# Attention scores by fp32 row tiles against bfloat16 splits through DRAM, in a kernel of two attentions and two MLPs

## The chip, the cores and the metric

The kernel runs on one core of a Trainium2 chip. Its engines run in parallel and meet by semaphores: TensorE (PE in the profile) multiplies into PSUM, which has 8 banks of 128 partitions x 512 fp32 numbers; VectorE (DVE), ScalarE (ACT) and GpSimd (POOL) work on tiles of 128 partitions; the DMA engines move data, and here nearly all DMAs are issued by SyncE (SP, its queue SPq). The metric is the device time of one execution in microseconds; lower is better. It was measured three times: 398.62 us (median), 397.15 us and 402.47 us.

## The reference

There are 16 batches of 128 rows x 256 numbers. Each goes through two rounds of attention and feed-forward, with a layer norm ahead of each part:

```python
x = x + _L0_xattn_ref(_layernorm(x), ctx, ctx)      # 16 heads of 16 numbers, causal, 128 queries x 128 keys
x = x + _L0_ffn_ref(_layernorm(x), ...)             # 256x256 layer plus the 2 best of 8 experts of rank 16
x = x + _L1_xattn_ref(_layernorm(x), ctx, ctx, g)   # 8 heads over the 128 rows as features, 256 queries x 256 keys
x = x + _L1_ffn_ref(_layernorm(x), w1, w2, gamma)   # 256 -> 1024, gelu, -> 256, activations rounded to 8 bits
```

Both attentions are softmax(q k / 4) v in fp32. Their scores need more precision than one bfloat16 product gives.

## The kernel before

Every batch b passes the same stages: attention 0, expert layer ("moe"), attention 1, MLP. The program is a pipeline over iterations t. The table of constants at the top (S0, S1T, EXP1 and so on) says how many iterations after its first one a batch reaches a stage, so that in iteration t each engine works on some ten batches at different stages. In every iteration an engine walks its own hand-written list (`fill` for t below 8, `body` to 15, `drain` after), and within that order only semaphores hold it back. One wait that isn't met holds all that stands behind it on the same engine.

**Scores.** Each fp32 operand is split into three bfloat16 parts. For k, POOL does four operations per batch (`k_high`, `k_rest_`, `k_mid`, `k_low`); for q, ACT makes a rounded and a full copy of the normalised rows and POOL takes the rests. The parts go out to DRAM (`k_parts`, `q0_parts`, `q1_parts`) and come back stacked, six parts of a head's 16 rows on 96 partitions (`load_stack`), so that one bfloat16 matmul over 96 rows gives the score of one head to nearly fp32 precision. `scores0` and `scores1` (L1166, L1197) compute scores with queries on the partitions, of which DVE takes row maxima (`maxima0`, `maxima1`, L1851). The negated maxima are split in two parts, turned by PE, copied by ACT and written by two DMAs (`rows0`, `rows1`, L755 and L764) as rows 96 and 97 of the stacked q, against two rows of ones in the stacked k. `scores0_t` and `scores1_t` (L1182, L1213) then compute the scores again with keys on the partitions and the maxima already subtracted, ACT takes the exponential into p (L1555, L1565), POOL sets the part above the diagonal to 0 in attention 0 (L920), and PE multiplies by v with an added column of ones (`pv0`, `pv1`, L1227, L1244). The causal mask is added to `scores0` by one bfloat16 matmul of 512 columns (L1162).

**PSUM.** A unit of scores is one bank, 512 columns wide; per batch there are 4 units in attention 0 and 8 in attention 1, in each of the two directions. `ps_s` has two banks and `ps_st` has two, used in turn, so PE can fill one while DVE or ACT reads the other.

**Tiles of TensorE.** The products by v have 32 output columns (L1227, L1244 say 128*32: rows*columns of the array), four such matmuls writing to four groups of 32 partitions. All other matmuls use the whole array.

**MLP.** Its stages have offsets of 16 to 31 iterations: layer-norm statistics and quantisation of the input (`stats3_` to `copy_in`), `up` (L1465), gelu (L1786), its maximum (L2274), rounding (`round_hid` L1796, `quant_hid` L2302), `turn_hid`, `copy_hid`, `down` (L1492), scaling and adding. The first gelu comes after the last exponential; ACT then loads its other function table once.

**Loads.** SP starts with x and kv of the first two batches, then the constants; the MLP weights are loaded by ACT's queue in iterations 4 and 6, the rest of x by ACT in iterations 0 to 5.

## Time and profile before

The profiled execution has a span of 399.2 us from its first to its last instruction, against the median of 398.62 us over the runs.

| | PE | DVE | ACT | POOL |
|---|---|---|---|---|
| busy, us | 306.1 | 315.5 | 262.4 | 271.7 |
| share of the span | 77% | 79% | 66% | 68% |

The DMA engines moved 56.21 MB at a mean of 141 GB/s. A busy engine is not an engine at its peak: a matmul's record lasts until its results are in PSUM, and the next one streams in behind it. "Idle before" is an engine's idle time just ahead of a group, with what released it. PEld is the loading of weights into the array, which runs beside matmuls.

### The profile page before, as it was taken

How to read it: one execution, taken by the hardware profiler on the slowest of the kernel's cores; microseconds unless marked ns; L12 is line 12 of the kernel's file. 1: busy time of each engine (PE TensorE's matmuls, PEld its weight loads, DVE VectorE, ACT ScalarE, POOL GpSimd, SP SyncE). 2: the span in 40 equal slices, each digit the busy share in tenths (PEclk: the TensorE clock that was granted, in tenths of full speed). 3: DMA queues.
4: the chain of work that ended last, by engine and by line, in shares of the span. 5: the costliest groups of instructions: out<-in, count | busy, mean ns of one | idle time of the engine just before them, and what ended most of it. 6: DMA issues, size and time to landing. Idle time of an engine off the chain costs nothing.

```text
span 399.2 us, 9590 instructions
## 1 busy us (share of the span) xinstructions
PE 306.1 (77%) x2926; PEld 192.0 (48%) x2946; DVE 315.5 (79%) x841; ACT 262.4 (66%) x501; POOL 271.7 (68%) x508
## 2 busy tenths in 40 slices
PE   0355665867989999898898899998777866767884
PEld 0233543654655656556555465555344432444553
DVE  6543579589898889899895889987797657999993
ACT  2422434636766887869576786596457548997993
POOL 5763988988988898699996795654542133756555
PEclk9999589869899999999998999999898889698998
DMA  5777768875866569567775667523444000000112
GB/s 185 188 222 225 185 168 253 240 177 159 187 183 201 153 180 251 152 196 175 203 218 129 187 160 203 132 64 84 96 108 118 14 16 1 0 16 29 40 54 79
DMA packets 73138, 56.21 MB, mean 141 GB/s; under 512 B 5376, under 2 KB 62592, under 8 KB 73088
## 3 DMA queue, kind: packets, MB, share of 16 engines
q1 hardware_dynamic: 69888, 51.67, 48.4%
q10 hardware_dynamic: 3200, 3.93, 3.3%
q8 instruction: 24, 0.39, 0.4%
q14 instruction: 26, 0.21, 0.2%
HBM read 36.45 MB, written 18.87 MB: 139 GB/s over the span
## 4 chain that ended last, share of the span: by engine, by line
PE 28%; POOL 19%; DVE 15%; issue 14%; DMA 12%; SPq 6%; ACT 4%; POOLq 1%; ACTq 0%; DVEq 0%
PE ps_u L1244 6%; DMA q<-max_t 5%; DVE max L1851 5%; PE ps_st L1213 4%; DMA kv_in<-in_kv 3%; PE ps_s L1197 3%; PE ps_ff L1314 3%; SPq L628 2%; POOL p L920 2%; POOL xs L1116 2%; PE ps_st L1182 2%; DMA k_parts<-k_split 2%; POOL rstd L970 2%; DVE hq L2302 1%; POOL k_split L853 1%
## 5 line engine op out<-in xcount | busy, mean ns | idle before, releaser
L1851 DVE TENSOR_REDUCE max<-ps_s 128x2 f32<-128x512 f32 (+1 forms) x192 | 127.0, 682 | 33.6 <-PE ps_s L1166 17.0
L1565 ACT ACTIVATE p<-ps_st 128x512 f32<-128x512 f32 x128 | 71.7, 599 | 18.7 <-PE ps_st L1213 16.9
L1213 PE MATMUL ps_st<-q,k 98*128 98x256 bf16 x256 | 47.9, 284 | 9.4 <-DMA q<-max_t 4.7
L1197 PE MATMUL ps_s<-k,q 96*128 96x256 bf16 x256 | 50.2, 283 | 5.4 <-DVE max L1851 2.5
L920 POOL TENSOR_SCALAR_AFFINE_SELECT p<-p 128x512 f32<-128x512 f32 x64 | 39.7, 636 | 8.1 <-ACT p L1555 8.0
L1555 ACT ACTIVATE p<-ps_st 128x512 f32<-128x512 f32 x64 | 35.6, 601 | 13.1 <-PE ps_st L1182 12.3
L1244 PE MATMUL ps_u<-p,v 128*32 128x256 f32 x512 | 38.0, 419 | 5.7 <-POOL v L910 5.7
L1213 PEld LDWEIGHTS ps_st<-q,k 98*128 98x128 bf16 x256 | 20.1, 100 | 31.5 <-DMA q<-max_t 9.2
L1166 PE MATMUL ps_s<-k,q 96*128 96x128 bf16 x256 | 27.2, 232 | 7.2 <-POOL p L920 6.4
L1569 ACT ACTIVATE q_split<-xs,shift,rstd 128x256 bf16<-128x256 f32 (+1 forms) x32 | 22.7, 711 | 12.4 <-POOL shift L972 8.1
L1081 POOL TENSOR_SCALAR amax_c<-amax,rms 128x1 f32<-128x1 f32 x16 | 4.9, 305 | 37.4 <-DVE amax L2256 37.3
L1182 PE MATMUL ps_st<-q,k 98*128 98x128 bf16 x256 | 27.2, 249 | 4.0 <-DMA q<-max_t 3.6
L1197 PEld LDWEIGHTS ps_s<-k,q 96*128 96x128 bf16 x256 | 20.8, 101 | 18.2 <-DVE max L1851 8.2
L1314 PE MATMUL ps_ff<-wff_sb,xh_t 128*128 128x392 f32 x64 | 26.5, 539 | 1.3 <-DVE w_mean L2098 0.8
L1166 PEld LDWEIGHTS ps_s<-k,q 96*128 96x128 bf16 x256 | 21.7, 105 | 9.9 <-issue 3.3
L1227 PE MATMUL ps_u<-p,v 128*32 128x128 f32 x512 | 25.2, 286 | 1.5 <-POOL p L920 1.3
L1182 PEld LDWEIGHTS ps_st<-q,k 98*128 98x128 bf16 x256 | 21.2, 113 | 9.4 <-DVE k L2154 3.0
L853 POOL TENSOR_SCALAR k_split<-kv_in 128x1024 bf16<-128x1024 f32 x14 | 14.6, 1045 | 16.2 <-DMA kv_in<-in_kv 9.1
L1342 PE MATMUL ps_t<-ident_bf,q_split 128*128 128x128 bf16 x128 | 13.3, 265 | 15.5 <-POOL q_split L943 15.5
L1244 PEld LDWEIGHTS ps_u<-p,v 128*32 128x32 f32 x512 | 14.4, 117 | 21.4 <-issue 10.3
L1796 ACT ACTIVATE hr<-hid,round_all,qscale 128x1024 f32<-128x1024 f32 x16 | 20.5, 1284 | 2.7 <-DVE qscale L2293 2.7
L1786 ACT ACTIVATE hid<-ps_s,dequant 128x512 f32<-128x512 f32 x32 | 20.8, 720 | 1.9 <-PE ps_s L1465 1.6
(144 smaller groups left out, 800.3 us busy)
## 6 DMA issues: line engine op xcount, KB each, us to landing
k_parts<-k_split SPq DMA_DIRECT2D x16, 512.0 KB, 4.8
k<-k_parts SPq DMA_DIRECT2D x32, 256.0 KB, 3.6
q<-q_parts SPq DMA_DIRECT2D x32, 256.0 KB, 4.0
kv_in<-in_kv SPq DMA_DIRECT2D x16, 256.0 KB, 3.9
q_parts<-q_t SPq DMA_DIRECT2D x16, 256.0 KB, 3.5
k<-k_parts SPq DMA_DIRECT2D x32, 128.0 KB, 3.6
q<-q_parts SPq DMA_DIRECT2D x32, 128.0 KB, 4.0
q_parts<-q_split SPq DMA_DIRECT2D x16, 256.0 KB, 3.1
```

Source lines behind the costliest of these rows:

```text
L920: pool.affine_select(out=kept, in_=kept, compare_op=ALU.is_ge, fill=0.0, base=0, pattern=[[0, G], [1, P]], channel_multiplier=-1).then_inc ...
L1166: last = pe.matmul(out_[:, j * P:(j + 1) * P], q0[0:STK, odd, c:c + P], k0[0:STK, odd, c:c + P], start=False, stop=(j == G - 1), skip_grou ...
L1182: last = pe.matmul(out_[:, j * P:(j + 1) * P], k0[0:STM, odd, c:c + P], q0[0:STM, odd, c:c + P], start=(j == 0), stop=True, skip_group_che ...
L1197: last = pe.matmul(out_[:, f * D:(f + 1) * D], q[0:STK, odd, h * D + f * P:h * D + (f + 1) * P], k[0:STK, odd, h * D:(h + 1) * D], start=( ...
L1213: last = pe.matmul(out_[:, f * D:(f + 1) * D], k[0:STM, odd, h * D + f * P:h * D + (f + 1) * P], q[0:STM, odd, h * D:(h + 1) * D], start=( ...
L1227: last = pe.matmul(ps_u[32 * j:32 * j + 32, g * P:(g + 1) * P], v0[:, odd, h, :], p0[:, g, j * P:(j + 1) * P], start=True, stop=True, skip ...
L1244: last = pe.matmul(ps_u[32 * j:32 * j + 32, g * D:(g + 1) * D], v1[:, f * H1 + h, :], p1[:, h, f * D:(f + 1) * D], start=(f == first), sto ...
L1314: last = pe.matmul(ps_ff[:, 0:NFF], xh1_t[:, f, :], wff_sb[:, f, :], start=(f == 0), stop=(f == FT - 1), skip_group_check=True)
L1555: act.activation(p0[:, g, :], ps_st[bank_of(ST_BANKS, f"s0t{g}")][:, :], ACT.Exp, scale=SCALE).then_inc(exp0_done[g], 1)
L1565: act.activation(p1[:, h, :], ps_st[bank_of(ST_BANKS, f"s1t{h}")][:, :], ACT.Exp, scale=SCALE).then_inc(exp1_done[h], 1)
L1569: return act.activation(out_, in_, ACT.Identity, scale=scale, bias=shift)
L1851: dve.tensor_reduce(out_, src, AX.X, ALU.max, negate=True).then_inc(done, 1)
```

## The change

The kernel is rewritten around one idea, and its parts are:

- **No splits.** q and k stay fp32. The array is used as four tiles of 32 rows x 128 columns. A row group of 32 partitions holds two heads; k has zeros where the other head's rows would be, so that one matmul over 32 rows with 256 columns gives the scores of two heads. The zeros are set once per buffer by DVE (`zero_k0`, `zero_k1`). `k_parts`, `q0_parts`, `q1_parts`, their stores and loads, and all of POOL's, ACT's and DVE's split operations on q and k are gone.
- **Loads of k.** `load_k0` and `load_k1` copy k from the input by 8 DMAs per batch each, of 16 partitions, on SP's queue.
- **Maxima.** They are still split in two (now by POOL), turned and copied, but are added from `max0_t` and `max1_t` by a bfloat16 matmul of 2 rows x 512 columns per bank; no DMA carries them.
- **Units of two banks.** `ps_s` and `ps_st` are each one buffer of two banks, 1024 columns. Per batch and direction there are 2 units in attention 0 and 4 in attention 1; maxima, exponentials and masks are 1024 wide. `claim` makes PE wait until the reader of the last unit is done with both banks.
- **Pairs.** `together` interleaves a transposed unit on two of the row groups with a plain unit of another batch on the other two.
- **Moved work.** x1, the index conversion and pick2 go from DVE to POOL. The MLP input stages of batches 0 to 12 are done between attentions.
- **MLPs in three groups.** Batches 0 to 5 after the scores of batch 13, 6 to 11 after the last exponential, and then 12 to 15, with hidden and input tiles in 7 buffers each.
- **Order and loads.** All iterations are written out. All loads are on SP: kv of three batches, x of the first, the constants, both MLP weights, the rest of x, and then k.

```diff
-        ps_s = [bank(f"ps_s{i}", [P, G * P]) for i in range(2)]
-        ps_st = [bank(f"ps_st{i}", [P, G * P]) for i in range(2)]
+        ps_s = bank("ps_s", [P, HALF, BANK])
+        ps_st = bank("ps_st", [P, HALF, BANK])
...
-            sp.dma_start(view[0:RUN], first_rows(parts)).then_inc(landed, 16)
-            sp.dma_start(view[RUN:STK], second_rows(parts, slot)).then_inc(landed, 16)
...
+                for i in range(I):
+                    for e in range(E):
+                        rows = slice(i * R + e * DH, i * R + (e + 1) * DH)
+                        sp.dma_start(k0[rows, n, :, e, :],
+                                     kv[b, rows, 0, :].rearrange("p (f l) -> p f l", f=FT)).then_inc(k0_landed[n], 16)
...
+            def together(*streams):
+
+                moved = {s: 0 for s in streams}
+                while moved:
+                    least = min(moved, key=moved.get)
+                    columns = next(least, None)
+                    if columns is None:
+                        del moved[least]
+                    else:
+                        moved[least] += columns
...
+            def scores0(b, h):
+                n = b % K0_BUFS
+                claim("s")
+                for m in range(HALF):
+                    pe.matmul(ps_s[:, m, :], ident_bf[:, :], mask_q[:, :, :].rearrange("p g k -> p (g k)"), start=True,
+                              stop=False, skip_group_check=True)
+                pe.wait_ge(k0_landed[n], (b // K0_BUFS + 1) * I * E * 16)
+                pe.wait_ge(q0_copied, b + 1)
                 for f in range(FT):
...
+                    for m in range(HALF):
+                        i = h * HALF + m
+                        rows = slice(i * R, (i + 1) * R)
+                        last = pe.matmul(ps_s[:, m, f * D:(f + 1) * D], q0[rows, b % Q_BUFS, f, :],
+                                         k0[rows, n, f, :, :].rearrange("p e l -> p (e l)"), start=False, stop=True,
+                                         skip_group_check=True)
...
+            def scores1_t(b, k, h):
+                n = b % K1_BUFS
+                claim("st")
+                pe.wait_ge(max1_copied, b + 1)
+                for e in range(E):
+                    for m in range(HALF):
+                        i = h * HALF + m
+                        rows = slice(i * R, (i + 1) * R)
+                        pe.matmul(ps_st[:, m, e * D:(e + 1) * D], k1[rows, n, e, k * P:(k + 1) * P], q1[rows, b % Q_BUFS, :],
+                                  start=(e == 0), stop=True, skip_group_check=True)
+                    yield D
+                for m in range(HALF):
+                    i = h * HALF + m
+                    pe.matmul(ps_st[:, m, :], ones_bf[i * R:i * R + 2, :],
+                              max1_t[i * R:i * R + 2, :, :, :].rearrange("p e f q -> p (e f q)"), start=False, stop=True,
+                              skip_group_check=True).then_inc(st1_ready[k][h], 1)
+                hold("st", (exp1_done[k][h], b + 1))
+                yield P
```

PE's order in the middle of the program before, at the start of an iteration of `body` (p and v are the probabilities and values, ps_u their product, ps_ut the turned product, ps_t the bank of small transposes):

```order
L1197 MATMUL ps_s0<-k1,q1 128x256 x2
L1244 MATMUL ps_u<-p1,v1 32x256 x8
L1213 MATMUL ps_st0<-q1,k1 128x256 x2
L1256 MATMUL ps_ut<-ident,u0 128x128 x4
L1213 MATMUL ps_st1<-q1,k1 128x256 x2
L1353 MATMUL ps_t<-ident,a1 128x128 x2
L1197 MATMUL ps_s1<-k1,q1 128x256 x2
L1213 MATMUL ps_st0<-q1,k1 128x256 x2
```

The same engine in the middle of the changed program, from the start of one batch's product by v (L1038 is `scores1`, L1019 and L1024 `scores0_t`, L1064 `scores1_t`, L984 and L992 `scores0`, L1101 `pv1`, L1164 the expert layer):

```order
L1164 MATMUL ps_ff<-wff_sb,xh1_t 128x392 x2
L1101 MATMUL ps_u<-p1,v1 32x256 x8
L1019 MATMUL ps_st<-q0,k0 128x128 x2
L1038 MATMUL ps_s<-k1,q1 128x512 x2
L1019 MATMUL ps_st<-q0,k0 128x128 x6
L1024 MATMUL ps_st<-max0_t,ones_bf 128x512 x2
L1051 MATMUL ps_t<-ident_bf,max1_split 128x128 x4
L1101 MATMUL ps_u<-p1,v1 32x256 x8
L1019 MATMUL ps_st<-q0,k0 128x128 x2
L1038 MATMUL ps_s<-k1,q1 128x512 x2
```

Units of one bank in alternating buffers became units of both banks in one buffer, and between two units stand matmuls on other tile shapes.

SP's queue at the start of the program before, up to the second batch's q:

```order
L652 DMA base_b_all<-in_base_b 128x256
L652 DMA wff_sb<-in_w_ff 128x2x392
L652 DMA router_b_all<-in_router_b 128x8
L676 DMA k_parts<-k_split 128x2x1024
L652 DMA lora_b_sb<-in_lora_b 128x256
L652 DMA attn_gamma_all<-in_attn_gamma 128x1
L652 DMA mlp_gamma_all<-in_mlp_gamma 128x256
L685 DMA q0_parts<-q0_t 128x1024
L627 DMA k0<-k_parts 64x8x256
```

The same queue in the changed program, from the weights on:

```order
L370 DMA w1_sb<-in_w1 128x1024 x2
L370 DMA w2_sb<-in_w2 128x4x256 x2
L320 DMA xs<-in_x 128x256
L320 DMA xs<-in_x 128x2x256 x2
L320 DMA xs<-in_x 128x4x256
L320 DMA xs<-in_x 128x6x256
L343 DMA k0<-in_kv 16x2x128 x24
L329 DMA kv_in<-in_kv 128x512 x3
L359 DMA k1<-in_kv 16x256 x40
L343 DMA k0<-in_kv 16x2x128 x16
```

The k of the first batch, which followed kv and some of the constants, now stands behind all weights and all of x, and the k of batch 3 (the first 8 of the last row) behind 24 + 3 + 40 other DMAs that follow x.

## Rows read from the trace of the kernel before

**Rows 1.** The page: busy time, share of the span and instructions of each engine:

```profile
PE 306.1 (77%) x2926; PEld 192.0 (48%) x2946; DVE 315.5 (79%) x841; ACT 262.4 (66%) x501; POOL 271.7 (68%) x508
```

**Rows 2.** Busy time (instructions) by stretch of the span, clock, DMA share, GB/s:

```profile
core 0: us, PE busy (x) PEld busy (x) DVE busy (x) ACT busy (x) POOL busy (x), PEclk, DMA share, GB/s
0.00:20.00 20.00, 3.29 (x23) 2.27 (x24) 12.45 (x28) 6.59 (x10) 13.13 (x36) 1.00 0.68 186
20.00:80.00 60.00, 38.56 (x361) 26.70 (x364) 35.15 (x86) 25.37 (x51) 45.21 (x75) 0.86 0.76 215
116.00:250.00 134.00, 122.93 (x1328) 78.14 (x1329) 116.04 (x326) 104.14 (x208) 109.17 (x183) 0.99 0.70 187
331.00:399.00 68.00, 46.54 (x364) 29.85 (x358) 57.59 (x134) 55.58 (x93) 39.52 (x86) 0.91 0.09 32
```

**Rows 3.** Single lines: count, shortest/median/longest ns, first and last start:

```profile
L1166 PE MATMUL ps_s<-k,q x256: 217/218/314, 19.1 to 256.3; 96*128 96x128 bf16 x128
...
L1197 PE MATMUL ps_s<-k,q x256: 269/273/421, 79.5 to 318.7; 96*128 96x256 bf16 x128
...
L1658 ACT COPY u<-ps_u x16: 577/587/588, 116.3 to 331.5; 128x512 f32<-128x512 f32 x16
...
L1658 ACT COPY u<-ps_u x6: 577/587/588, 147.9 to 231.5; 128x512 f32<-128x512 f32 x6
...
L1786 ACT ACTIVATE hid<-ps_s,dequant x32: 677/690/830, 335.1 to 387.1; 128x512 f32<-128x512 f32 x32
```

**Rows 4.** The page: the chain that ended last, share of the span by engine:

```profile
PE 28%; POOL 19%; DVE 15%; issue 14%; DMA 12%; SPq 6%; ACT 4%; POOLq 1%; ACTq 0%; DVEq 0%
```

**Rows 5.** Groups by form: count | busy us, mean ns | idle before, releasers:

```profile
L1851 DVE TENSOR_REDUCE max<-ps_s 128x2 f32<-128x512 f32 x128 | 84.9, 683 | 16.5 <-PE ps_s L1197 16.2
L1565 ACT ACTIVATE p<-ps_st 128x512 f32<-128x512 f32 x128 | 71.7, 599 | 18.7 <-PE ps_st L1213 16.9 <-issue 0.2
...
L1796 ACT ACTIVATE hr<-hid,round_all,qscale 128x1024 f32<-128x1024 f32 x16 | 20.5, 1284 | 2.7 <-DVE qscale L2293 2.7
L2274 DVE TENSOR_REDUCE amax<-hid 128x1 f32<-128x1024 f32 x16 | 19.2, 1202 | 0.6 <-ACT hid L1786 0.4
```

**Rows 6.** PE in time: start, us, line, array rows*columns, shapes, count:

```profile
206.04 0.38 PE L1162 MATMUL ps_s<-mask_q,ident_bf 128*128 128x512 bf16 x1
206.25 0.39 PE L1166 MATMUL ps_s<-k,q 96*128 96x128 bf16 x4
206.57 0.67 PE L1227 MATMUL ps_u<-p,v 128*32 128x128 f32 x16
207.17 0.60 PE L1314 MATMUL ps_ff<-wff_sb,xh_t 128*128 128x392 f32 x1
...
217.42 0.60 PE L1268 MATMUL ps_ut<-ident,u 128*128 128x128 f32 x4
```

**Rows 7.** PE in time: sixteen records of the second product by v:

```profile
129.08 1.07 PE L1244 MATMUL ps_u<-p,v 128*32 128x256 f32 x16
```

**Rows 8.** SP queue in time: start, us that the issue took, transfer:

```profile
8.91 1.10 SPq L652 DMA_DIRECT2D mlp_gamma_all<-in_mlp_gamma  x1
...
12.57 0.69 SPq L627 DMA_DIRECT2D k<-k_parts  x1
13.32 0.61 SPq L628 DMA_DIRECT2D k<-k_parts  x1
...
205.46 0.35 SPq L649 DMA_DIRECT2D kv_in<-in_kv  x1
```

**Rows 9.** The DMAs of the maxima rows: shortest/median/longest ns of an issue:

```profile
L755 SPq DMA_DIRECT2D q<-max_t x32: 548/580/689, 24.2 to 259.9; - x32
```

**Rows 10.** The page: GB/s of the DMA engines in 40 slices:

```profile
GB/s 185 188 222 225 185 168 253 240 177 159 187 183 201 153 180 251 152 196 175 203 218 129 187 160 203 132 64 84 96 108 118 14 16 1 0 16 29 40 54 79
```

**Rows 11.** ACT in time, late in the MLPs:

```profile
378.05 1.34 ACT L1786 ACTIVATE hid<-ps_s,dequant 128x512 f32<-128x512 f32 x2
...
380.95 1.37 ACT L1786 ACTIVATE hid<-ps_s,dequant 128x512 f32<-128x512 f32 x2
```

More of the change, by code:

```diff
@@ L33 @@
 FT = D // P
+R = 32
+I = P // R
+HALF = I // 2
+E = R // DH
+BANK = 512
 NE = 8
@@ L256, in kind @@
-def kind(t):
-    return 1 if not isinstance(t, int) or FILL <= t < NB else 0 if t < FILL else 2
-def in_turn(units, b, back=0):
-    stages, orders = units
-    which = [kind(b - back + stage) if isinstance(b, int) else 1 for stage in stages]
-    return sorted(range(len(stages)), key=lambda n: (stages[n], orders[which[n]].index(n)))
+X_GROUPS = ((0, 1), (1, 2), (2, 4), (4, 6), (6, 10), (10, NB))
+KV_BUFS = 3
+K0_BUFS = 3
+K1_BUFS = 5
+V0_BUFS = 3
+V1_BUFS = 5
+Q_BUFS = 2
+XN_BUFS = 4
+XR_BUFS = 3
@@ L536, in program @@
         xq_copied = sem("xq_copied")
-        hid_ready = sem("hid_ready")
+        hid_ready = [sem(f"hid_ready{n}") for n in range(2)]
         gelu_done = [sem(f"gelu_done{n}") for n in range(2)]
@@ L590, in claim @@
-        def claim(engine, bank):
-            for sem_, value in held.get(bank, ()):
-                engine.wait_ge(sem_, value)
-        def take(engine, order, banks, user, t):
-            bank_ = order[0][0], [name for name, _ in order].index(user) % banks
-            if isinstance(t, int):
-                claim(engine, bank_)
-            else:
-                name, last = before(order, banks, user, t)
-                engine.wait_ge(freed[name], last + 1)
-            if isinstance(t, int):
-                held[bank_] = ((freed[user], t - dict(order)[user] + 1),)
@@ new lines, in _ @@
+            turn_gated(3)
+            pv0(5, 0)
+            pv0(5, 1)
+            together(scores1_t(1, 0, 0), scores1(2, 1, 1))
+            turn_u0(5)
+            turn_q0(7)
+            together(scores1_t(1, 1, 0), scores0(6, 1))
+            lora(3)
+            turn_back(0)
+            together(scores1_t(1, 1, 1), scores1(2, 1, 0))
+            turn_max0(6)
+            ff(4)
+            pv1(1, 0)
+            together(scores0_t(6, 1), scores1(3, 0, 0))
+            turn_max1(2)
+            pv1(1, 1)
@@ new lines, in _ @@
+            turn_gated(6)
+            pv0(8, 0)
+            pv0(8, 1)
+            together(scores1_t(4, 0, 0), scores1(5, 1, 1))
+            turn_u0(8)
+            turn_q0(10)
+            together(scores1_t(4, 1, 0), scores0(9, 1))
+            lora(6)
+            turn_back(3)
+            together(scores1_t(4, 1, 1), scores1(5, 1, 0))
+            turn_max0(9)
+            ff(7)
+            pv1(4, 0)
+            together(scores0_t(9, 1), scores1(6, 0, 0))
+            turn_max1(5)
+            pv1(4, 1)
```

3823 lines of the change are left out of this document (2267 added, 1556 removed).

## The prediction

> **What bounds the kernel now.** First the page's busy shares: PE 77%, DVE 79%, POOL 68%, ACT 66% of 399.2 us [rows 1]. No engine is full, and the chain that ended last is shared out, PE 28%, POOL 19%, DVE 15%, DMA 12%, waits for issues 14% [rows 4]. So nothing bounds it alone; look by stretch [rows 2]. Until 80 us PE is busy for 42 of 80 us while the DMA engines move 186 to 215 GB/s, and no slice of the page has more than 253 [rows 11]: a fill held by transfers and POOL. From 116 to 250 us PE is busy 92% and DVE 87%. From 331 us there are only MLPs, 68 us.
>
> Three markers divide the time [rows 3]: `scores0` first runs at 19.1, `scores1` at 79.5, and ACT copies the second product by v (u, once per batch) at 116.3 for the first batch and 331.5 for the last. Six starts of it between 147.9 and 231.5 are five periods: 16.7 us per batch in the full pipeline. The first gelu is at 335.1.
>
> How long PE streams is read from spacing, not from mean ns. Four bfloat16 matmuls of 128 columns occupy 206.25 to 206.64 with their tail of .17, so .055 each, one column per cycle at 2.4 GHz [rows 6]. Sixteen records of 256 columns in fp32 take 1.07 us [rows 7]. They are 8 matmuls of two records each, on four column tiles. Four records per tile in (1.07 - .17) / 4 = .22 us each is two cycles per column, and the four tiles run side by side. So an fp32 matmul of N columns costs 4N cycles, .43 us for 256, .86 for 512.
>
> **The change, part by part.**
>
> Scores on PE. Before, a batch has 12 units in each of two directions, 512 bfloat16 columns each, .21: 24 x .21 = 5.1 us. After, it has 6 units of two banks per direction. In a pair each of the four row groups streams 512 fp32 columns, .86, and one bfloat16 matmul of 512 for the maxima, .21: 1.07 if the four run side by side, as the column tiles do. Six pairs are 6.4 us. The masks are .86 (two units x 2 x .21). So PE's scores cost 1.5 to 2 us more per batch, for half as many instructions. No row shows row tiles; the bounds are below.
>
> A rule speaks against the 1.07: the Trainium skill, "TensorE: Matmul & The Clock Gate", Part 3, reports 3.07 times, not 4, for four row tiles with K = 32 and 512 columns. By it the .86 would be an estimated 4 x .86 / 3.07 = 1.12, and 81 pairs would add 21 us. No run here shows it yet, and the sum does not use it.
>
> Switches of tile shape. Between the last 128-row matmul and the first column tile PE pauses about .10 (206.47 to 206.57), and back again .17 (207.00 to 207.17) [rows 6]. Before there are about 5 per batch. In the new order one steady iteration passes between row tiles, column tiles and the whole array 18 times. At .16 that is 2.9 us.
>
> The rest of PE's iteration: `pv1` 1.7 and `pv0` .9, the expert layer 1.3 (2 x .327 x 2 for 392 columns), turning u .9, lora .4, turns of xh, a and q .65, gated .1, maxima .4: 6.4 us. Sum: 6.4 + .9 + 6.4 + 2.9 = 16.6 us of PE per batch.
>
> One buffer instead of two. PE may start a unit only when its reader has finished both banks. DVE's maximum over 1024 columns takes 1.20 (the row of that size), against 2 x .68; ACT's exponential of 1024 between 2 x .60 and, by the form of that width, 1.28 [rows 5]. From a pair's last column to the next pair's first: .17 tail + 1.20 + .1 = 1.45 us. Pair plus hand-over is 2.5 us, so PE cannot take fewer than 6 x 2.5 = 15.1 per batch. PE's other work, (16.6 - 6.4) / 6 = 1.7 per pair, would cover 1.45 if spread evenly; it is not: `pv1`, the expert layer and the turns stand in three of six gaps. I charge half a microsecond in each of the other three: 1.5. A steady iteration is 16.6 + 1.5 = 18.1 us, against 16.7. Bounds: 15.6 (hand-over alone, with half a microsecond of slack) and 20.
>
> What is taken from others. DVE goes from 12 maxima at .68 to 6 at 1.20 and gives x1 and index work to POOL; POOL gives up the splits; ACT the copies. DMA traffic falls from 56 MB to some 15 (an estimate: inputs, kv of each batch twice, output). I cost all this at nothing in the middle, because PE's own iteration is longer than theirs, and it gives nothing either. Without that cover DVE's 7 us of maxima plus the rest still stay under 14.
>
> SP's queue in the fill. The first k0 stands behind kv, the constants, both weights and x, 5.6 MB. At the best rate seen, 253 GB/s, that is 22 us, plus issue of 8 DMAs and 2 us of flight: first scores at 26 (19.1 before). Then SP issues 24 + 3 + 40 + 8 DMAs before the k of batch 3 is complete. Issues over 128 partitions take .35 [rows 8]; those of other shapes .61 and .69 (same rows), of the 16-partition maxima .58 [rows 9]; behind a backlog 1.10. With 16 partitions the nearest is .58, plus .06 between: .64. 72 x .64 + 3 x .4 = 47 us after 19.5: k of batch 3 is there at 67. PE reaches it after 10 units that are not in pairs; each is 1.07 plus 1.45 of hand-over of which units in the other direction cover some, I take 2.2: at 26 + 22 = 48. So PE, whose list is in one order, stands for 19 us, and behind it everything.
>
> From 67 on: 7 units of 2.9 (18.1 / 6 is 3.0, the fill has fewer pairs): first `scores1` at 87 (before 79.5); 9 units to the first `pv1` at 113 (before about 115); 6 units, 17 us, to the second at 130; nine full iterations to `pv1` of batch 10: 9 x 18.1 = 163, at 293. Then 25 units, 13 of them pairs, of 2.7: 361.
>
> MLPs. The first group of six stands before that: 12 gelus that PE, ACT and DVE would otherwise do later, and two more changes of ACT's function table; the hand-over units run on, so I charge only part of it: 18 us. Last `pv1` at 379 (before 331.5). Behind it stand 10 MLPs, not 16. Late in the program a batch takes 2.9 us (378.05 to 380.95) [rows 10]: 10 x 2.9 = 29, plus 12 for the way of the last batch through all stages, 41 (before 68).
>
> Sum: 26 + 22 + 19 + 20 + 26 + 17 + 163 + 68 + 18 + 41 = **420 us**. The profile is of 399.2 against a median of 398.62, so nothing is to be corrected.
>
> **Rivals.**
>
> *Faster (about 375).* Hand-over alone sets the pace, 15.6 us, because PE's small work fits the gaps; switches cost .05. For it: PE only needs 13.7 without switches, and all other engines get lighter. Then 9 x 2.5 = 22 less, the late units 2.4 instead of 2.7, 8 less, and with cheap issues 17 less: 373. It decides on the faster side once an iteration is below 16.5 with a short stall. Chance .22.
>
> *Within 2% (391 to 407).* The small DMAs are issued in .39 like those of 128 partitions. Then k of batch 3 is there at 19.5 + 72 x .39 + 1 + 2, about 50, and the stall of 19 is 2: 403. Or the stall stands and an iteration is 16.8. Against it: every row of fewer than 128 partitions says .58 or more. Chance .18.
>
> *Row tiles less parallel (470 to 495).* If only two run at once, 81 pairs cost 1.07 more: 420 + 87, less what hand-overs hide, 495. If their weights are loaded one after another, a pair with 20 loads of .1 has 1 us exposed in half of the cases, 460. Against it: column tiles are fully parallel [rows 7]. Chance .12.
>
> *As forecast, 407 to 450:* .48.
>
> **How the numbers follow.** The forecast is 420, the likeliest case. The range leaves out part of the fast and most of the row-tile case: 383 to 462. 2% is about what a measurement of this kernel can tell from no change. Faster .22, same .18, slower .48 + .12 = .60.
>
> **What would show it.** SP's rows for k0 and k1: issue near .6 or near .4, and PE's idle time ahead of the `scores0` of batch 3. The period of the u copy in the middle: 18.1, and its parts: records of a pair (1.07 side by side), the gaps where the tile shape changes, and PE's idle time ahead of `ps_s` and `ps_st`, put down to DVE's maximum or ACT's exponential. First `scores0` at 26, `scores1` at 87, last u copy at 379. I am wrong if PE is seldom idle and the period is below 16.7, if the stall is short, or if the row groups' records follow one another.

## The result, and the profile after

The changed kernel takes 428.01 us (median of 5 runs, 423.12 to 429.85) against 401.35 us for the kernel before, measured beside it: a ratio of 1.068, with a 95% interval of 1.058 to 1.077. Medians here and below are of all executions, while ratios and their intervals leave out executions in the chip's slower state, more than 1.5% above the fastest of their kernel. The forecast was 420. The profiled execution is the shortest of the five (423.12 us) and has a span of 421.3 us; all stretches below are of it, and the forecast's sum compares with its 421.3.

From the page of the changed kernel: busy shares, the chain's shares, and the groups of the exponential and the maximum.

```profile
PE 347.9 (83%) x3634; PEld 205.3 (49%) x3634; DVE 284.5 (68%) x633; ACT 238.8 (57%) x375; POOL 188.2 (45%) x436
...
PE 63%; ACT 13%; issue 8%; SPq 6%; DVE 6%; POOL 2%; DMA 1%; ACTq 0%; POOLq 0%; DVEq 0%
...
L1744 ACT ACTIVATE p<-ps_st 128x1024 f32<-128x1024 f32 x64 | 65.5, 1024 | 78.0 <-PE ps_st L1069 78.0
L2210 DVE TENSOR_REDUCE max<-ps_s 128x4 f32<-128x1024 f32 x64 | 78.3, 1223 | 41.5 <-PE ps_s L1038 40.6
```

PE is now the busiest engine by far (83%, where [rows 1] had 77%) and 63% of the chain, against 28% in [rows 4]. DVE, ACT and POOL all have less work than before, and the kernel is slower all the same. The same views of single lines as in [rows 3] (count, shortest/median/longest ns, first and last start): `scores0`, `scores1`, the copy of the second product by v (u) over the whole run and within 140 to 240 us, and SP's loads of the first attention's k.

```profile
L992 PE MATMUL ps_s<-k,q x256: 374/374/792, 23.7 to 287.6; 32*128 32x256 f32 x128
...
L1038 PE MATMUL ps_s<-k,q x256: 587/662/1052, 79.6 to 356.6; 32*128 32x512 f32 x128
...
L1753 ACT COPY u<-ps_u x16: 576/603/604, 107.8 to 378.3; 128x512 f32<-128x512 f32 x16
...
L1753 ACT COPY u<-ps_u x6: 603/603/604, 144.6 to 239.3; 128x512 f32<-128x512 f32 x6
...
L343 SPq DMA_DIRECT2D k<-in_kv x128: 311/423/1999, 15.1 to 244.7; - x128
```

And the stretches, with the columns of [rows 2]:

```profile
0.00:24.00 24.00, 1.86 (x6) 0.92 (x8) 10.03 (x25) 3.06 (x5) 8.20 (x30) 1.00 0.74 250
24.00:60.00 36.00, 27.25 (x190) 15.94 (x188) 22.20 (x42) 12.57 (x16) 13.39 (x26) 1.00 0.18 51
...
291.00:374.00 83.00, 73.14 (x711) 43.22 (x709) 59.55 (x136) 59.21 (x92) 30.55 (x77) 0.98 0.04 11
```

The period of the u copy in the middle is (239.3 - 144.6) / 5 = 18.94 us, where [rows 3] give 16.7. By the same copy the two profiled executions compare as follows. The first copy comes 8.5 us earlier (107.8 against 116.3). The ten periods behind it take 185.5 us against 159.7, and the last five, among which the first group of MLPs now stands, 85.0 against 55.5. Behind the last copy (378.3 against 331.5) stand 43.0 us instead of 67.7. Together that is 22.1 us more.

| step | forecast | measured |
|---|---|---|
| first `scores0` | 26 | 23.7 |
| to that of batch 3 | 41 (22, and a stall of 19) | 36 |
| to the first `scores1` | 20 | 20 |
| to the first `pv1` | 26 | 23 |
| to the second | 17 | 19 |
| nine iterations | 163 | 169 |
| to the last `pv1` | 86 (68 + 18) | 83 |
| rest | 41 | 47 |
| sum | 420 | 421 |

The first seven rows go by PE's starts of the score units and of `pv1`. For its last `pv1` the prediction's 379 took over a marker of [rows 3] that is the start of the u copy (331.5 before); by that marker it was 378.3, with 43 us behind it, against 379 and 41.

One pair in the middle shows what an iteration is made of. The rows are of PE, DVE and ACT (weight loads left out); the pair runs from 207.33 to 208.61, where a full-array transpose starts.

```profile
207.33 0.48 PE L1064 MATMUL ps_st<-q,k 32*128 32x256 f32 x2
...
207.47 0.70 PE L1038 MATMUL ps_s<-k,q 32*128 32x512 f32 x2
...
208.01 0.59 PE L1038 MATMUL ps_s<-k,q 32*128 32x512 f32 x2
...
208.61 0.66 PE L1113 MATMUL ps_ut<-ident,u 128*128 128x128 f32 x4
208.74 1.23 DVE L2210 TENSOR_REDUCE max<-ps_s 128x4 f32<-128x1024 f32 x1 [1.32 <-PE ps_s L1038]
208.83 1.02 ACT L1744 ACTIVATE p<-ps_st 128x1024 f32<-128x1024 f32 x1 [0.81 <-PE ps_st L1069]
...
209.91 0.70 PE L1064 MATMUL ps_st<-q,k 32*128 32x256 f32 x4 [0.42 <-ACT p L1744]
210.54 0.61 PE L984 MATMUL ps_s<-mask_q,ident_bf 128*128 128x512 bf16 x2
...
212.14 0.70 PE L1181 MATMUL ps_ff<-lora_b_sb,gated_t 128*128 128x256 f32 x2
...
213.49 0.48 PE L1064 MATMUL ps_st<-q,k 32*128 32x256 f32 x2 [0.43 <-ACT p L1744]
...
222.69 0.70 PE L1064 MATMUL ps_st<-q,k 32*128 32x256 f32 x4 [0.40 <-ACT p L1680]
```

Two units on four row groups stand in 1.28 us, a gap of .10 at the change of tile shape included. DVE reads `ps_s` from 208.74 for 1.23 us, ACT reads `ps_st` from 208.83 for 1.02. PE has .9 us of other work, waits .42 for ACT, and starts the next transposed unit at 209.91. The mask matmul of the plain unit that is paired with it starts at 210.54. It does not wait for DVE, whose maximum ended at 209.97: it stands behind the transposed unit's first four records in PE's list. That pair, with its masks, takes 2.23 us (209.91 to 212.14). There are three waits per iteration, .40 to .43 each, and all three are for ACT's exponential.

### The profile page after: what moved, and what is told of

It is laid out like the page before. It is cut to its first block, busy times and chain, and to the rows that moved or that the text cites. A ratio compares the mean times of both kernels' runs of the same rounds, so it can differ in the third digit from the quotient of the medians.

```text
span 421.3 us, 10475 instructions
## 1 busy us (share of the span) xinstructions
PE 347.9 (83%) x3634; PEld 205.3 (49%) x3634; DVE 284.5 (68%) x633; ACT 238.8 (57%) x375; POOL 188.2 (45%) x436
## 4 chain that ended last, share of the span: by engine, by line
PE 63%; ACT 13%; issue 8%; SPq 6%; DVE 6%; POOL 2%; DMA 1%; ACTq 0%; POOLq 0%; DVEq 0%
PE ps_st L1064 11%; PE ps_u L1101 7%; PE ps_s L992 7%; ACT p L1744 6%; PE ps_st L1019 6%; PE ps_s L1038 6%; PE ps_ff L1164 5%; PE ps_s L984 4%; PE ps_u L1086 4%; ACT p L1680 3%; PE ps_st L1069 3%; SPq L343 3%; ACT hid L1788 2%; PE ps_u L1223 2%; SPq L320 1%
## 5 line engine op out<-in xcount | busy, mean ns | idle before, releaser
L1744 ACT ACTIVATE p<-ps_st 128x1024 f32<-128x1024 f32 x64 | 65.5, 1024 | 78.0 <-PE ps_st L1069 78.0
L2210 DVE TENSOR_REDUCE max<-ps_s 128x4 f32<-128x1024 f32 x64 | 78.3, 1223 | 41.5 <-PE ps_s L1038 40.6
L1064 PE MATMUL ps_st<-q,k 32*128 32x256 f32 x512 | 78.3, 411 | 16.7 <-ACT p L1744 11.9
L1038 PE MATMUL ps_s<-k,q 32*128 32x512 f32 x256 | 72.9, 644 | 1.8 <-DVE max L2210 1.8
L2201 DVE TENSOR_REDUCE max<-ps_s 128x8 f32<-128x1024 f32 x32 | 39.2, 1225 | 41.6 <-PE ps_s L992 41.6
L1064 PEld LDWEIGHTS ps_st<-q,k 32*128 32x128 f32 x512 | 42.4, 184 | 32.9 <-ACT p L1744 22.3
L992 PE MATMUL ps_s<-k,q 32*128 32x256 f32 x256 | 41.9, 450 | 12.7 <-DMA k<-in_kv 12.7
L1680 ACT ACTIVATE p<-ps_st 128x1024 f32<-128x1024 f32 x32 | 32.8, 1024 | 28.0 <-PE ps_st L1024 28.0
L508 POOL TENSOR_SCALAR_AFFINE_SELECT p<-p 128x1024 f32<-128x1024 f32 x32 | 35.2, 1101 | 16.6 <-ACT p L1680 16.6
L1019 PE MATMUL ps_st<-q,k 32*128 32x128 f32 x512 | 41.3, 303 | 1.4 <-ACT p L1680 1.2
L1019 PEld LDWEIGHTS ps_st<-q,k 32*128 32x128 f32 x512 | 34.5, 203 | 11.1 <-ACT p L1680 6.0
L992 PEld LDWEIGHTS ps_s<-k,q 32*128 32x128 f32 x256 | 24.8, 209 | 30.1 <-issue 15.2
L1101 PE MATMUL ps_u<-p,v 128*32 128x256 f32 x512 | 33.6, 384 | 0.0
L1164 PE MATMUL ps_ff<-wff_sb,xh_t 128*128 128x392 f32 x64 | 24.8, 510 | 0.0
L984 PE MATMUL ps_s<-mask_q,ident_bf 128*128 128x512 bf16 x64 | 22.0, 430 | 2.3 <-DVE max L2201 2.3
L1223 PE MATMUL ps_u<-w_q,hq_t 128*128 128x256 bf16 x128 | 16.7, 273 | 6.3 <-DVE hq_t L2436 4.8
L1038 PEld LDWEIGHTS ps_s<-k,q 32*128 32x128 f32 x256 | 19.7, 183 | 3.9 <-DVE max L2210 2.7
```

What stands on the lines that cost most here:

```text
L984: pe.matmul(ps_s[:, m, :], ident_bf[:, :], mask_q[:, :, :].rearrange("p g k -> p (g k)"), start=True, stop=False, skip_group_check=True)
L992: last = pe.matmul(ps_s[:, m, f * D:(f + 1) * D], q0[rows, b % Q_BUFS, f, :], k0[rows, n, f, :, :].rearrange("p e l -> p (e l)"), start=Fa ...
L1019: pe.matmul(ps_st[:, m, c * P:(c + 1) * P], k0[rows, n, f, e, :], q0[rows, b % Q_BUFS, f, :], start=(c == 0), stop=True, skip_group_check= ...
L1038: pe.matmul(ps_s[:, m, :], q1[rows, b % Q_BUFS, f * P:(f + 1) * P], k1[rows, n, :, :].rearrange("p e l -> p (e l)"), start=True, stop=True ...
L1064: pe.matmul(ps_st[:, m, e * D:(e + 1) * D], k1[rows, n, e, k * P:(k + 1) * P], q1[rows, b % Q_BUFS, :], start=(e == 0), stop=True, skip_gr ...
L1101: last = pe.matmul(ps_u[R * j:R * (j + 1), h * D:(h + 1) * D], v1[:, b % V1_BUFS, k * H1 + h * G + j, :], p1[:, k, h * HALF + m, e, :], st ...
```

## The experiments

All changes below are to the changed kernel unless it says otherwise. Times are medians; the ratio is to the kernel before.

**Are the row tiles of a pair side by side?** The two units one after another:

```diff
-                moved = {s: 0 for s in streams}
-                while moved:
...
+                for stream in streams:
+                    for _ in stream:
+                        pass
```

> Same matmuls, but the two units of each of the 81 pairs stand one after another instead of interleaved, so that only two of the four row groups are busy at once. Theory A (the four row groups of a pair really run side by side): each pair costs about 1.0 us more, of which the readers' waits (1.6 us per iteration) disappear; period about 23, total about 485. Theory B (the row groups of a pair partly queue behind one another anyway): period under 21, total under 460.

449.2 us (two executions), ratio 1.120 (1.109 to 1.131). It is slower by 21 us, not by the 57 of theory A. The numbers of theory B held (period 20.5, total under 460), but the rows refute its mechanism. One such pair on PE (L1014 and L1019 are the transposed unit, L1033 the plain one, L1046 the next work on the whole array):

```profile
210.86 0.94 PE L1014 MATMUL ps_st<-q,k 32*128 32x128 f32 x12
211.53 0.70 PE L1033 MATMUL ps_s<-k,q 32*128 32x512 f32 x2
...
211.85 0.38 PE L1019 MATMUL ps_st<-max_t,ones_bf 2*128 2x512 bf16 x2
212.06 0.59 PE L1033 MATMUL ps_s<-k,q 32*128 32x512 f32 x2
212.59 0.40 PE L1046 MATMUL ps_t<-ident_bf,max_split 128*128 128x128 bf16 x4
```

From 210.86 to 212.59 are 1.73 us instead of 1.28 to 1.31. The plain unit does not wait until the transposed one has ended: its first two records start at 211.53, while the other two row groups still stream. So row groups overlap even when they are listed one unit after the other. What the interleaving saves is .45 us here, and .65 for a pair with masks at 216.50 in this trace (2.88 against 2.23). The period is 20.5 us, 1.5 more. I had charged a full 1.0 per pair, as if the second unit began after the first one's end.

The changed kernel itself has a direct comparison. Late in it a transposed unit stands alone, on two row groups:

```profile
304.32 1.13 PE L1064 MATMUL ps_st<-q,k 32*128 32x256 f32 x8
...
305.60 1.58 PE L1164 MATMUL ps_ff<-wff_sb,xh_t 128*128 128x392 f32 x4
```

It takes 1.28 us to the next work on the whole array, as long as the pair of two units on four row groups from 207.33. The second unit of a pair costs PE nothing.

**Are PE's waits those of readers of the one buffer?** Maxima and exponentials read only half of the columns, so the output is not the reference's and only the time counts:

```diff
-                                  ps_s[:, :, :].rearrange("p m (c k) -> p (m c) k", k=P), AX.X, ALU.max,
+                                  ps_s[:, :, :].rearrange("p m (c k) -> p (m c) k", k=P)[:, :, 0:P // 2], AX.X, ALU.max,
...
-                               ps_st[:, :, :].rearrange("p m c -> p (m c)"), ACT.Exp, scale=SCALE)
+                               ps_st[:, :, :].rearrange("p m (c q) -> p (m c) q", q=P)[:, :, 0:P // 2], ACT.Exp, scale=SCALE)
```

> DVE's maxima and ACT's exponentials read only half of the columns of each unit (the other half of p is set to 1 once at the start, some 10 us of DVE's idle time in the fill), so the output is not the reference's; PE's list is unchanged. Theory A (PE's three waits per iteration, 1.65 us, are for the one buffer per direction to be read): the waits vanish, period 17.2 to 17.5, which is PE's streaming plus its shape switches; total 400 to 410. Theory B (they are waits for something else and would stay): period above 18.5, total above 420.

396.8 us, ratio .989 (.984 to .995). The u copy from 140 to 240 us, and the groups of DVE's maximum and ACT's exponential (count | busy, mean ns | idle before):

```profile
L1756 ACT COPY u<-ps_u x5: 586/586/586, 153.8 to 224.0; 128x512 f32<-128x512 f32 x5
...
L2213 DVE TENSOR_REDUCE max<-ps_s 128x4 f32<-128x512 f32 x64 | 44.2, 691 | 53.5 <-PE ps_s L1039 53.2
...
L1747 ACT ACTIVATE p<-ps_st 128x512 f32<-128x512 f32 x64 | 38.2, 597 | 72.7 <-PE ps_st L1070 72.6
```

The period is (224.0 - 153.8) / 4 = 17.55 us, 1.4 less, with PE's list untouched, and PE's waits for the readers are gone from the middle: theory A. The total of 396.8 is below the 400 to 410 that it said. Of the 27 us between the two profiled executions 5.7 lie ahead of the first u copy (102.1 instead of 107.8), 12.9 in the ten periods behind it, 8.6 in the last five and none behind the last one (43 us in both). So the readers' time is also paid in the fill and in the late units. In the median it is 31 us, the largest single effect that the runs separate: with readers at half width the changed kernel is no slower than the one before. The kernel before was not run with such readers, so how much they would give there is open.

**Does covering the waits with other work help?** The lora product one pair earlier, the expert layer one earlier:

```diff
+            lora(5)
             together(scores1_t(3, 1, 0), scores0(8, 1))
-            lora(5)
             turn_back(2)
+            ff(6)
             together(scores1_t(3, 1, 1), scores1(4, 1, 0))
             turn_max0(8)
-            ff(6)
```

> In nine middle iterations PE does the lora product before the fifth pair of the iteration and the next batch's expert layer before the sixth (both stood one place later), and DVE's moe_out goes ahead of one maximum. Theory A (PE waits .4 us ahead of the fifth and sixth pair because too little small work stands between the pairs to cover ACT's exponential of 1.02 us on the one ps_st buffer): period of the u copy from 18.93 to about 18.15, total about 421. Theory B (the wait only moves to the places that lost work): period 18.8 to 19.0, total 428.

427.0 us, ratio 1.062 (1.053 to 1.071): theory B. The u copy, then PE's rows at the places:

```profile
L1753 ACT COPY u<-ps_u x5: 605/607/607, 148.5 to 223.8; 128x512 f32<-128x512 f32 x5
...
207.35 0.70 PE L1064 MATMUL ps_st<-q,k 32*128 32x256 f32 x4 [0.47 <-ACT p L1680]
...
220.55 0.49 PE L1019 MATMUL ps_st<-q,k 32*128 32x128 f32 x4 [0.44 <-ACT max_t L1672]
```

The period is (223.8 - 148.5) / 4 = 18.8. Two of the three waits for ACT's exponential are gone. The one at 207.35 stays, and the wait of .44 at 220.55 is new: the turned maxima are copied by ACT behind an exponential, and the expert layer had covered that. Moving this work about mostly moves the wait.

**What does PE's own streaming cost?** q stored in bfloat16, k read through its upper 16 bits:

```diff
-        q1 = sb("q1", [P, Q_BUFS, D])
+        q1 = sb("q1", [P, Q_BUFS, D], BF16)
...
-                              k1[rows, n, :, :].rearrange("p e l -> p (e l)"), start=True, stop=True,
+                              high(k1[rows, n, :, :].rearrange("p e l -> p (e l)")), start=True, stop=True,
```

> q is stored in bfloat16 and k read through its upper 16 bits, in all four kinds of score matmul (so the scores have only bfloat16 precision); everything else stands. Theory A (the middle is 2.2 us per iteration slower than before because of PE's streaming of fp32 columns, 6 x .86 us): a pair of units takes about .5 instead of 1.28 us, PE's streaming falls from 14.9 to about 10.5 us per iteration, and the period from 18.93 to 14 to 15.5, where DVE's 13.7 us of busy time and the readers' hand-over are next; total 375 to 390. Theory B (hand-over and switches of tile shape set the pace, streaming is hidden in them): period 17.5 or more, total above 405.

406.5 us (two executions), ratio 1.012 (1.001 to 1.023). Theory A's 375 to 390 was missed; the period of (226.5 - 155.9) / 4 = 17.65 and the total are those of theory B. The u copy, PE in time, the stretch from 150 to 250 us and two single periods (columns as in [rows 2]), and PE's longest wait from 150 to 250 us (us in total, times, longest):

```profile
L1756 ACT COPY u<-ps_u x5: 599/599/603, 155.9 to 226.5; 128x512 f32<-128x512 f32 x5
...
187.24 0.23 PE L1022 MATMUL ps_st<-q,k 32*128 32x128 bf16 x2
...
192.39 0.38 PE L987 MATMUL ps_s<-mask_q,ident_bf 128*128 128x512 bf16 x1 [0.16 <-issue]
...
200.18 0.63 PE L987 MATMUL ps_s<-mask_q,ident_bf 128*128 128x512 bf16 x1 [0.33 <-ACT q L1667]
...
150.00:250.00 100.00, 80.68 (x857) 39.51 (x866) 75.94 (x178) 61.79 (x100) 55.28 (x127) 0.88 0.12 29
...
172.90:189.50 16.60, 12.79 (x155) 6.40 (x157) 13.63 (x32) 11.17 (x20) 9.53 (x23) 1.00 0.12 33
189.50:210.70 21.20, 18.23 (x163) 8.96 (x167) 14.12 (x32) 11.30 (x19) 10.28 (x24) 0.68 0.11 27
...
PE ps_t L1177 <- DVE gated L2294: 8.1, 6, 1.5
```

The pair did become short: from 187.24 to 187.79, .55 us. But the same mask matmul takes .38 us at 192.39 and .63 at 200.18: PE alternates between the levels of 2.4 and 1.2 GHz, the granted clock of the stretch is .88 where it was 1.00, and PE, with less to do between its waits, is busy only 81%. That agrees with the Trainium skill, "TensorE: Matmul & The Clock Gate", Part 1: a kernel with short idle times between groups of matmuls was seen to oscillate between the two levels. The lower clock does not come from the bfloat16 operands as such: the kernel before, with bfloat16 scores and PE busy 92% of its middle, had .99 [rows 2]. The four periods took 17.0, 16.6, 21.2 and 15.8 us at granted clocks of .90, 1.00, .68 and 1.00. So at the full clock a period is about 16.2, and of 6 x (1.28 - .55) = 4.4 us less streaming some 2.7 were a gain; the clock took 1.4 of it back on the mean. The rest went into a wait that the changed kernel does not have in its middle: PE stands for DVE's `gated` of the expert layer, 8.1 us in 100. Its waits for the readers (7.1 in 100) are as long as before.

**Masks.** The maximum over all keys serves a softmax as well:

```diff
-                for m in range(HALF):
-                    pe.matmul(ps_s[:, m, :], ident_bf[:, :], mask_q[:, :, :].rearrange("p g k -> p (g k)"), start=True,
-                              stop=False, skip_group_check=True)
```

> The two mask matmuls of 128x512 ahead of each scores0 unit are left out (row maxima are then taken over all keys, which any softmax allows; the part above the diagonal of p is still set to 0 by POOL). Per iteration that is 4 matmuls, .86 us of streaming, and four changes of tile shape at about .1. Theory A (PE's sum is the period: whatever leaves PE's list shortens it): period from 18.93 to 17.6 to 17.9, total about 414. Theory B (the masks stand where PE would wait for ACT's exponential and DVE's maximum anyway): period 18.6 to 18.9, total 425 to 428.

411.6 us, ratio 1.028 (1.019 to 1.038). The u copy, and on PE the pair that had the masks:

```profile
L1750 ACT COPY u<-ps_u x6: 605/606/606, 141.7 to 229.0; 128x512 f32<-128x512 f32 x6
...
202.15 0.48 PE L1061 MATMUL ps_st<-q,k 32*128 32x256 f32 x2 [0.40 <-ACT p L1741]
...
203.43 0.70 PE L1178 MATMUL ps_ff<-lora_b_sb,gated_t 128*128 128x256 f32 x2
```

The period is (229.0 - 141.7) / 5 = 17.46, 1.48 less: theory A, by a little more than it said. The pair takes 1.28 us where it took 2.23 with its masks, so the masks cost PE 1.9 us per iteration: .86 of streaming, some .4 for four changes of tile shape, and the rest because the transposed unit's first half streams alone ahead of the masks. Not all of it shows in the period, because a wait of some .5 us for DVE's `gated` appears. This is the fastest form of the changed kernel whose scores are all computed and read in fp32. With bfloat16 reading added:

> bfloat16 reading of q and k and no mask matmuls (scores with bfloat16 precision). Theory A (the readers' hand-over is the pace once PE streams little: six times .17 + 1.23 + .1 plus a short pair of .5 and the work that cannot lie in a hand-over): period 15.5 to 16.5, total 390 to 398. Theory B (PE's clock falls the more, the less PE has to do, and takes the gain back): granted clock below .9, slow records in over a third of the time, period 17 or more, total 400 to 410.

400.9 us, ratio 1.002 (.999 to 1.005).

```profile
150.00:250.00 100.00, 80.55 (x870) 42.90 (x870) 76.08 (x170) 62.07 (x100) 53.21 (x120) 0.80 0.10 28
```

Theory B: granted clock .80, PE still 81% busy with less work, period (223.0 - 151.5) / 4 = 17.9. What PE no longer had to do went into its clock and into the wait for `gated`, now 12.1 us of these 100; the run does not separate the two.

**The kernel before without its masks.** The same edit there (four matmuls of 512 columns per batch):

> The kernel before, with the one mask matmul of 128x512 ahead of each of its scores0 units left out (maxima over all keys, as in the run of the changed kernel without masks). Theory A (PE, busy 92% of the middle, gives up 4 x .21 us per batch and part of it shows in the period): period of the u copy from 16.7 to 15.9 to 16.3, total 388 to 396, below both kernels. Theory B (with two buffers per direction PE has slack at these places; the waits for POOL and DMA elsewhere take it up): period 16.5 to 16.7, total 397 to 401.

398.8 us against 401.9 of the kernel before, ratio .986 (.980 to .992). 

```profile
L1656 ACT COPY u<-ps_u x6: 579/587/587, 147.5 to 227.8; 128x512 f32<-128x512 f32 x6
```

The period is (227.8 - 147.5) / 5 = 16.06, theory A. But these five periods are the better part: from the first u copy to the last it is 213.3 us against 215.2 before. The medians differ by .8%, and the total of 398.8 is above the 388 to 396 of theory A. It is probably faster than the kernel before, by about 1%, which is less than the 2% that such a measurement can tell from no change.

**The MLPs.** The first group of six behind the last exponential, on all four engines; the calls are the same:

```diff
-            up(0, 0)
-            up(0, 1)
...
             together(scores1_t(15, 1, 1))
             turn_in(11)
+            up(0, 0)
+            up(0, 1)
...
             pv1(15, 0)
```

> The first group of MLPs (batches 0 to 5), from its first matmul to its output, moves from between the last attentions to just behind the last exponential on PE, ACT, DVE and POOL; input tiles in 16 buffers. Theory A (the group costs about as much where it stands, 18 us by the prediction, as 6 x 2.9 = 17 us at the end): last pv1 about 15 us earlier, total within 4 us of 428. Theory B (between the attentions it hides in waits of PE and ACT): total 434 or more. Theory C (two changes of ACT's table and the gelus in the way of exponentials make it dearer there than at the end): total 418 or less.

455.0 us, ratio 1.129 (1.117 to 1.142): theory B, and by more than it said. The profiled execution is the longest of the four (461.1, left out of the ratio; the others took 451.2 to 457.7), so its stretches show where the time went and overstate it. Two of them:

```profile
343.00:363.00 20.00, 16.63 (x110) 8.55 (x102) 7.87 (x15) 6.18 (x9) 1.85 (x6) 0.60 0.00 0
363.00:415.00 52.00, 38.00 (x212) 19.62 (x210) 19.70 (x36) 26.14 (x37) 9.40 (x22) 0.64 0.05 16
```

The u copy of batch 14 comes at 363 us, and in the changed kernel at 364: taken out of the middle, the group gave back only a few microseconds, even allowing for a start that was 3 to 4 us later here (from the eleventh u copy to that of batch 14 it was 66.0 us, against 70.7). And the 20 us ahead of 363 ran at a granted clock of .60, where the changed kernel has 1.00 from 343 to 363, so the gain was measured at a lower clock. At the end the group cost some 37: from 363 to 415 PE, busy 38 of 52 us, waits for gelu, rounding and copies in turn, and its granted clock is .64. One part is of my making: `pv1` of batch 15 had to stand behind the group (its bank serves `up` too), so batch 15 was late as well. How much of the 27 us is that and how much the clock, the run does not tell.

**The fill.** The forecast had a stall of SP. What the queue really did (start, us for the row's issues):

```profile
29.27 20.65 SPq L359 DMA_DIRECT2D k<-in_kv  x40
50.03 3.63 SPq L343 DMA_DIRECT2D k<-in_kv  x8
```

An issue of 16 partitions takes .42 us (the median in the L343 row above), not .58: 40 in 20.65 us, .52 apart with waits. The k of batch 3 was issued from 50.03 to 53.66, eight DMAs, and was there at about 55 (the page has a median of 1.7 us from issue to landing). PE reached it only at 60.0, without a wait. A PE that came at 48, as forecast, would have stood for some 7 us. It came late because it waited 8.8 us of those 36 for POOL's splits and DVE's maxima, and because its records were twice as long as later. PE's rows in the fill, and a unit of as many columns at 87.93:

```profile
23.66 2.08 PE L992 MATMUL ps_s<-k,q 32*128 32x256 f32 x8 [12.70 <-DMA k<-in_kv]
```

```profile
87.93 1.13 PE L1038 MATMUL ps_s<-k,q 32*128 32x512 f32 x4
```

The eight records of a unit take 2.08 us, which is the length of the 1.2 GHz level, against 1.13 for a unit of the same columns later. All of PE's rows until 57 us are long in this way, though the granted clock of the stretch is given as 1.00; ahead of them PE had done six matmuls in 24 us. Four runs changed the fill, three by the order of loads and lists and one by keeping PE busy.

> Only the order of SP's queue at the start changes: kv and x of batch 0, k of batch 0, x of batches 1 and on, constants, k of batch 1, then the weights and the rest (and DVE zeroes k0's first buffer first). Theory A (the first k starts a chain that all later work follows): first scores0 at about 11 us instead of 23.7, first scores1 8 to 12 us earlier than 79.6, total about 418. Theory B (the fill is held by something later, such as the path max -> split -> turn -> copy of each batch, and by weights that now come later): first scores0 early, but first scores1 within 3 us of 79.6 and total 425 to 428.

425.6 us, ratio 1.065 (1.054 to 1.075): theory B. The first `scores0` moved to 9.5 us, and the first `scores1` stayed (80.7 against 79.6). DVE in that run:

```profile
24.39 0.75 DVE L2191 BATCH_NORM_STATS2 stats<-xs 128x6 f32<-128x256 f32 x2 [15.53 <-DMA xs<-in_x]
```

The first maximum stood behind statistics of x that now landed at 24.39: one wait of an in-order list took the other's place.

```diff
+            def keep_busy(n):
+                for _ in range(n):
+                    pe.matmul(ps_u[:, :], ident_bf[:, :], mask_q[:, :, :].rearrange("p g k -> p (g k)"), start=True,
+                              stop=True, skip_group_check=True)
```

> Nothing is taken out; PE gets 55 matmuls of 128x512 bf16 into a bank that nobody reads, while it waits for the first k, and 8 each in its next two waits. In the changed kernel all of PE's records until 57 us take twice the time they take later (a pair of units 2.1 us against 1.1). Theory A (the slow level of PE's clock costs the fill its time, and comes from PE having been nearly idle before): records from 24 us on at the fast level, scores0 of batch 3 at about 52 instead of 60.0, total about 420. Theory B (the clock is slow for another reason or other engines set the pace there): scores0 of batch 3 at 59 to 61, total 427 to 429.

424.5 us, ratio 1.059 (1.050 to 1.068), between the two theories.

```profile
24.67 1.13 PE L992 MATMUL ps_s<-k,q 32*128 32x256 f32 x8
...
27.80 2.07 PE L992 MATMUL ps_s<-k,q 32*128 32x256 f32 x8
```

After 54 such matmuls, from 10.54 to 24.3, the first unit runs at the upper level (1.13 us). PE then waits 1.44 us for DVE, and the second unit is back at 2.07. From 34 to 42 us the records are short again, from 45 to 68 long. Batch 3's `scores0` came 2 us earlier, at 58.0, and the first `scores1` at 81.8. So the stretches that this run made fast bought little. What the full clock through the whole fill would give was not measured.

> Only the start is reordered, on four engines at once: SP loads x and k of batch 0, then of 1 and 2, before constants and weights; DVE takes the maxima of batches 0 to 2 before the statistics of later x and before the sums of the MLP weights; POOL splits the maxima of batches 0 and 1 before it places v of batches 3 and 4; the weight rounding of ACT, DVE and PE comes after batch 3's maxima. Theory A (the fill is a chain max, split, turn, copy per batch, held by what stands ahead of it in the lists of DVE and POOL, and not by SP alone): scores0 of batch 3 at 40 to 48 instead of 60.0, first scores1 at 65 to 70 instead of 79.6, total 408 to 415. Theory B (PE's slow clock level, left at 57 to 70 us in all runs so far, holds the fill whatever the order): scores0 of batch 3 after 52, first scores1 after 75, total above 420.

430.0 us, ratio 1.072 (1.063 to 1.082). This run loads x and k of batches 0 to 2 first and takes their maxima and splits ahead of other work. Batch 3 came at 44.0, as theory A said, but the first `scores1` at 80.6 and the total are those of theory B: PE stood 4 us for the sums of the MLP weights, which I had put into its way, and 4 us for `gated`.

> As the first reordering of the fill (x and k of batches 0 to 2 ahead of constants and weights; DVE and POOL take the maxima first), but the work on the MLP weights, for which PE waited 4 us from 52 us on in that run, is spread: their sums between the maxima of batch 3, ACT's rounding and DVE's clipping behind the exponentials of batches 3 and 4. Theory A (the 16 us gained up to batch 3 were lost again only at that work): first scores1 at 65 to 72 instead of 79.6 and total 410 to 418. Theory B (the gain is lost between batch 3 and the first scores1 whatever stands there, at PE's slow clock level and in the chain attention, expert layer, attention of batch 0): first scores1 after 77, total above 424.

431.6 us, ratio 1.078 (1.065 to 1.092), with the work on the MLP weights spread out.

```profile
62.15 0.61 PE L1006 MATMUL ps_t<-ident_bf,max_split 128*128 128x128 bf16 x4 [5.43 <-POOL max_split L523]
...
78.88 0.70 PE L1038 MATMUL ps_s<-k,q 32*128 32x512 f32 x2 [0.30 <-ACT q L1647]
```

Batch 3 at 45.0 again, first `scores1` at 78.9, theory B. PE now stood 5 us for a split of maxima by POOL at 62.15. In the four runs the first `scores1` came at 78.9 to 81.8. What would bring it earlier I have not found.

## Why the prediction was right

**Sign and size.** 420 forecast, 421.3 in the profiled execution and 428 as a median. The longer executions had granted clocks of .955 to .979, the profiled one .993; the sum had no term for that.

**Iteration: right, two terms too small.** 18.1 forecast, 18.94 measured. The hand-over was right in size (1.45 forecast; 1.40 from the last column, at 208.51, to 209.91) and in number (three waits of .40 to .43 where I charged three of .5), but it is ACT's exponential that ends it, not DVE's maximum, from which the prediction had worked it out. The half-width readers show that it is worth 1.4 us per iteration. The pair's 1.07 was mis-sized: it is 1.18, which is .66 per iteration. The rows show where the .11 is: the second 512-column record of a row group starts .54 after the first (207.47, 208.01), not .43. It is not that four row groups hinder one another, for the lone unit at 304.32 takes the same 1.18. By the rule weighed in the prediction (3.07 times for four row tiles, "TensorE: Matmul & The Clock Gate", Part 3, the Trainium skill) a pair would be an estimated 1.33; 1.18 less .21 for the maxima is .97 for four times .86, which is 3.5 times. The rule and the sum are each about as far off. The pairs (.66) and the masks (.4, below), less waits of 1.25 where 1.5 was charged, make the missing .8 us, and this is the 6 us between 163 and 169.

**Masks: a little small.** I took .86 for four matmuls and, among the 18 switches of .16, four of theirs: 1.5 in all. They cost PE 2 x (2.23 - 1.28) = 1.9, of which the run without them shows 1.48 in the period.

**SP's stall: wrong.** It was the term of 19. The step that failed is "With 16 partitions the nearest is .58": they take .42, and the k of batch 3 was there at about 55, not 67, before PE. The step beside it was wrong in the other direction, "I take 2.2" per unit, where 3.6 passed per unit: records twice as long for all of PE's work, and between them the waits for POOL's splits and DVE's maxima. How the 14 us divide between these two no run separates. The two errors nearly cancel, 41 against 36, and that is luck. The rival "within 2%" rested on the stall being absent, and it was absent without that result.

**MLPs: sum right, parts uncertain.** I charged 18 for the first group between the attentions, and 83 us passed there in all for the forecast's 86. Moving the group away gave back only some 5 us, but at a lower clock. If 5 is right, the 25 units took 78 us, 3.1 each and not 2.7, and the sum of 86 was luck as well. Behind the last u copy it was 43, forecast 41.

**Rivals.** That hand-over alone sets a pace of 15.6 was excluded: with half-width readers and no waits the iteration is still 17.55, which is PE's own sum. That row groups queue behind one another was excluded by the lone unit that takes as long as a pair. One variant stands untested: row tiles with units of one bank and two buffers per direction, as before. The two late references of the prediction are swapped: its 253 GB/s is in [rows 10], its 378.05 to 380.95 in [rows 11].

## What to carry over

When operands grow so that a unit needs all buffers of its kind, price the reader's time as part of the producer's loop: here it was 1.4 us of 18.9 in the steady state, and it was paid in the fill and in the late units too. The one reordering that was tried won back .1 us of it, because a copy behind the reader then came last. Before a fill is sped up by an earlier load, look at what stands ahead of the consumer in each in-order list; three reorderings moved the first step by up to 16 us and the end by nothing. And taking work off TensorE may not pay in full. Without the masks it stayed 91% busy at a granted clock of 1.00 and kept most of the gain; both versions with bfloat16 reading left it 81% busy and lost part of it to a clock of .88 and .80, and to the next wait in line.

## What the hardware showed that I had not expected

- DMAs of 16 partitions are issued in .42 us, not in the .58 to .69 of the other narrow ones in [rows 8, 9].
- A unit alone on two row groups takes as long as two units on four (1.28 us at 304.32 and at 207.33).
- Matmuls on different row groups overlap even when one unit's are all listed ahead of the other's (start of the second unit at 211.53, while the first ran on to 212.2).
- In the fill, records of the length of 1.2 GHz stand for 33 us under a granted clock of 1.00 in the stretch's row; in the middle of the bfloat16 runs the granted clock does show it (.88 and .80).
